# Masked cross attention: the key stack as two 64-row halves, three stacks in rotation, unrolled rounds

## The chip, the cores and the metric

The kernel runs on one NeuronCore of a Trainium2 chip, as one program in one launch. The metric is the device time of one execution in microseconds. TensorE (PE, with its weight loads as PEld) multiplies into PSUM; VectorE (DVE), ScalarE (ACT) and GpSimd (POOL) read PSUM and SBUF; SyncE (SP) only issues DMA transfers, all of them in one queue. Each engine works through its own instructions in order and waits on semaphores.

## The reference, cut to what matters

The program is a two-layer perceiver block over 16 batches of 64 tokens with 128 channels. The change touches one stage, the masked cross attention of layer 1 (`L1_xattn`), and the buffers around it:

```python
q = split_heads(x @ cq_w + cq_b)            # x: 16 x 64 x 128, 16 heads of 8
k = split_heads(ctx @ ck_w + ck_b)          # ctx: 16 x 1601 x 128
v = split_heads(ctx @ cv_w + cv_b)
scores = einsum('bqhd,bkhd->bhqk', q, k) / sqrt(8) + mask      # mask: 16 x 1 x 1 x 1601
probs = softmax(scores, axis=-1)
out = einsum('bhqk,bkhd->bqhd', probs, v)
```

The other stages (cross attention and self attention of layer 0, expert networks, self attention, quantised attention) are left as they are.

## The kernel before, in words

Everything of the stage is done per batch. The keys of a batch (128 channels x 1601) are projected in four chunks (512, 512, 512, 65 columns) and split into a rounded part `kh` (ACT) and a rest `kl` (DVE), so that fast fp32r multiplications keep fp32 accuracy. A stack `KS` (128 partitions x 4 groups x 1602) then holds, for each group g of four heads, `kh`, `kh` and `kl` of the group's 32 channels in partitions 0 to 95, and above them rows for the maximum and the mask. The queries are stacked in the same way (`QS`) and spread over heads by POOL (`QB`). One multiplication of a stack with `QB` gives scores that include mask and minus the maximum.

For each batch two passes over the scores are made. The first gives maxima: 8 head pairs x 4 key chunks = 32 matmuls in the layout queries x keys, each into PSUM bank 0 or 1 in turn, each reduced by one DVE instruction (line 1516). The maxima of a batch are then combined, transposed on PE (`nm`, line 1264), split into `nmh` and `nml` and sent by two small DMAs (line 897) into two rows of `QB`. The second pass gives scores in the layout keys x queries, 13 tiles of keys (steps k = 0 to 12): four matmuls into a pair of banks (2-3 or 4-5 in turn), one exponential on ACT into `PT` (line 1112), and eight column-tiled matmuls with the values (`values`).

The stage runs in slots n = -2 to 16, each of 13 steps. In slot n, PE does step k of batch n, and beside it the maxima of batch n+1 (0, 0, 3, 4, 4, 4, 4, 4, 4, 5, 0, 0, 0 of them in steps 0 to 12), and one side task per step through bank 7: `sum` of batch n-1 in step 1 (DVE takes its reciprocal, line 1499), the value projections `v0` to `v3` of batch n+1 in steps 2 to 5, the key projections `k0` to `k3` of batch n+2 in steps 6 to 9, and `nm` in step 10. A side task waits until bank 7 has been read by the one before it.

There are two stacks, `KS0` and `KS1`. The stack of batch n+1 is filled in slot n by SP (`sync_slot`): when the last scores of batch n-1 are done, one mask transfer and twelve transfers of 32 partitions x 1601 elements, in the order of the groups (`kh`, `kh`, `kl` for g = 0, then for g = 1, and so on); PE waits for a group before that group's first maximum. Behind them in SP's queue stand the load of the next context into `ctxT` and then the two small maxima transfers. Slots 2 to 11 are a loop of five rounds (`Fori`) with register arithmetic for semaphore values and addresses; the others are written out.

Of the kernel before, what the change touches and what calls it, by code (L numbers as in the profile page):

```python
# [16 lines left out]
HEADS, HD = 16, 8  # L17
# [36 lines left out]
def build(nc, A, out, mask_parts):  # L54
    ctx = ExitStack()
    with ctx:
# [25 lines left out]
        W["L1_xattn_fi_w"] = sb("w_fi", [128, FF])  # L82
        W["L1_xattn_fo_w"] = sb("w_fo", [128, FC, 128])
# [11 lines left out]
        for name in ("L0_xattn_bv", "L1_xattn_sv_b", "L1_xattn_co_b", "L1_xattn_co_g", "L1_xattn_co_be",  # L95
# [11 lines left out]
        qT = sb("qT", [128, 128])  # L107
# [16 lines left out]
        WqT = sb("WqT", [128, 128])  # L124
        WvT = sb("WvT", [128, 128])
# [3 lines left out]
        pc_sb = sb("pc_sb", [128, 128])  # L129
        pcT = sb("pcT", [128, 128])  # L130
# [33 lines left out]
        onT = expert_area[:, 0:2 * TOKENS].rearrange("p (r t) -> p r t", r=2)  # L164
# [6 lines left out]
        split_x = [q[:, :] for q in QB]  # L171
# [23 lines left out]
        LANE[0].update(q=qT[:, :], smax=smax[:, :], ssum=ssum[:, :])  # L195
        LANE[1].update(q=o_sb[:, :], smax=sb("smax1", [128, HEADS])[:, :], ssum=sb("ssum1", [128, HEADS])[:, :])
# [530 lines left out]
        MAXIMA = [(p, c) for p in range(8) for c in CS]  # L727
# [6 lines left out]
        progress("max_p", [f"m{p}{c}" for p, c in MAXIMA] + ["nm"])  # L734
        progress("max_v", [f"m{p}{c}" for p, c in MAXIMA] + ["nm", "nmh", "nml"])
# [15 lines left out]
        mask_stacked = sem("mask_stacked")  # L751
        ctxT_loaded = [sem(f"ctxT_loaded{q}") for q in range(2)]
        qs_stacked = sem("qs_stacked")
        ks_stacked = [sem(f"ks_stacked{g}") for g in range(4)]
        nm_stacked = sem("nm_stacked")
        mask_split = sem("mask_split")
# [27 lines left out]
        for name, t in W.items():  # L784
            src = A[name]
            if name == "L1_xattn_fo_w":
                src = src.rearrange("(c p) n -> p c n", p=128)
            elif name == "L1_attn_in_w":
                src = src.rearrange("(c p) n -> p c n", p=128)
            WLOADS.append((t, src))  # L790
# [11 lines left out]
        def slots(eng, slot):  # L802


            for n in (-2, -1, 0, 1):
                slot(n, n % 2)
            with eng.Fori(0, 5) as i:
                slot(2 * i + 2, 0)
                slot(2 * i + 3, 1)
            for n in (12, 13, 14, 15, 16):  # L810
                slot(n, n % 2)

        BESIDE = {k: ([], None) for k in range(KT)}
        for k, side, count in SCHEDULE:
            first = sum(len(b[0]) for b in BESIDE.values())
            maxima = ["m%d%d" % MAXIMA[m] for m in range(first, first + count)]
            BESIDE[k] = (maxima, side)
        IN_BANK7 = ["sum", "v0", "v1", "v2", "v3", "k0", "k1", "k2", "k3", "nm"]  # L820

        def present(item, n):
            c = isinstance(n, int)
            if item == "sum":
                return not (c and n < 1)
            if item[0] == "k":
                return not (c and n > 13)
            return not (c and (n < -1 or n > 14))

        def maxima(n, k, part=None):  # L830

            m = [item for item in BESIDE[k][0] if present(item, n)]
            return m if part is None else (m[:2], m[2:])[part]

        def side(n, k):

            item = BESIDE[k][1]
            return [item] if item and present(item, n) else []

        def bank7_free(item, n):  # L840

            before = [b for b in IN_BANK7[:IN_BANK7.index(item)] if present(b, n)]
            if before:
                last, m = before[-1], n
            elif isinstance(n, int) and n == 16:
                last, m = "sum", 15
            elif isinstance(n, int) and n == -1:
                last, m = "k3", -2
            elif isinstance(n, int) and n < -1:
                return  # L850
            else:
                last, m = "nm", n - 1
            if last == "sum":
                at(nc.tensor, "sum_v", "sum", m - 1)
            elif last[0] == "v":
                at(nc.tensor, "vals_a", last, m + 1)
            elif last[0] == "k":
                at(nc.tensor, "keys_v", "kl" + last[1], m + 2)
            else:
                at(nc.tensor, "max_v", "nml", m + 1)  # L860
# [13 lines left out]

        def sync_slot(n, q):

            c = isinstance(n, int)
            if not (c and n > 14):
                stack = KS[1 - q]
                if c and n <= 0:  # L880
# [798 lines left out]
```

## Time and profile before

| what | value |
|---|---|
| median of 3 runs | 1426.14 us (1424.24 to 1427.14) |
| the profiled execution | 1429.34 us, its span 1427.6 us |
| PE busy | 1091.4 us (76%) |
| DVE busy | 759.6 us (53%) |
| ACT busy | 482.5 us (34%) |
| POOL busy | 227.4 us (16%) |
| hardware DMA queue | 96.48 MB, 25.2% of 16 engines' span |
| chain of waits | PE 49%, issue 18%, DVE 14%, SP's queue 6%, DMA 5%, POOL 5%, ACT 2% |

The stage of the change reaches from about 412 us (the last expert result of layer 0) to about 1027 us of the span. The table is an average over all stages; within the slots PE is busy about nine tenths of the time at full clock, and the DMA engines are busy in the first 13 us of a slot's 34 and nearly idle in the rest. A busy PE row counts matmuls from issue to modelled end, so it is not PE at its peak.

### The profile page before, as it was taken

The page shows a single profiled execution, that of the slowest core. Times are in us where ns is not written, and L with a number is a line of the kernel's source. Part 1 is how long each engine was busy: PE and PEld are TensorE (multiplying, and loading weights), DVE is VectorE, ACT ScalarE, POOL GpSimd, SP SyncE. Part 2 cuts the span into 40 slices and gives each one's busy share as a digit, 9 for nine tenths or more (in the row PEclk, how much of TensorE's full clock was granted, in tenths as well). Part 3 has the DMA queues.
Part 4 walks back from the last instruction along what each step waited for, and adds up shares of the span by engine and source line. Part 5 has one row for each costly group of instructions (what it writes and reads, how often), then busy time and mean ns, then how long its engine had stood idle before and what let it go on. Part 6 is the DMA issues. An engine that isn't in the chain of part 4 may idle for free.

```text
span 1427.6 us, 24169 instructions
## 1 busy us (share of the span) xinstructions
PE 1091.4 (76%) x9246; PEld 795.1 (56%) x9246; DVE 759.6 (53%) x1498; ACT 482.5 (34%) x632; POOL 227.4 (16%) x232
## 2 busy tenths in 40 slices
PE   3677774899862798988898888988758625838987
PEld 1445463777741466666666666666536413536776
DVE  3224766343342566666666666666176377955112
ACT  0225221232220245455445455554414101402333
POOL 2000412121221011111111111111133003301110
PEclk9889876999985799999999999999879766857999
DMA  8581010101104344443444343433000000010111
GB/s 270 209 326 52 1 44 1 45 22 44 68 0 105 90 103 99 97 95 94 98 111 94 94 94 94 94 72 72 2 0 1 1 0 1 0 30 16 30 30 29
DMA packets 43611, 97.30 MB, mean 68 GB/s; under 512 B 12392, under 2 KB 27376, under 8 KB 43552
## 3 DMA queue, kind: packets, MB, share of 16 engines
q1 hardware_dynamic: 43552, 96.48, 25.2%
q8 instruction: 42, 0.69, 0.2%
q14 instruction: 17, 0.14, 0.0%
HBM read 54.67 MB, written 0.73 MB: 39 GB/s over the span
## 4 chain that ended last, share of the span: by engine, by line
PE 49%; issue 18%; DVE 14%; SPq 6%; DMA 5%; POOL 5%; ACT 2%; DVEq 0%; POOLq 0%; ACTq 0%
PE PS L262 47%; DVE mx L1516 3%; DMA KS<-kl 3%; DVE kl L1505 2%; SPq L913 2%; POOL work_area L390 2%; DVE u_all L275 1%; SPq L897 1%; DMA ctxT<-in_ctx_T 1%; POOL PT L390 1%; SPq L889 1%; DVE x L675 1%; DMA QB<-nml 1%; POOL blank_g L257 1%; POOL rstd_all L281 1%
## 5 line engine op out<-in xcount | busy, mean ns | idle before, releaser
L1516 DVE TENSOR_REDUCE mx<-PS 128x1 f32<-128x512 f32 (+1 forms) x512 | 278.5, 571 | 100.5 <-PE PS L262 93.0
L1112 ACT ACTIVATE PT<-PS 128x1024 f32<-128x1024 f32 (+1 forms) x208 | 212.4, 1022 | 64.6 <-PE PS L262 64.6
L262 PE MATMUL PS<-KS,QB 128*128 128x512 f32 (+1 forms) x512 | 178.8, 419 | 41.0 <-DVE mx L1516 22.0
L262 PE MATMUL PS<-QB,KS 128*128 128x256 f32 (+1 forms) x832 | 166.7, 323 | 18.1 <-DMA QB<-nml 18.1
L262 PE MATMUL PS<-QB,QS 128*128 128x512 f32 x576 | 157.5, 421 | 23.9 <-DVE wcol L663 21.7
L262 PEld LDWEIGHTS PS<-QB,KS 128*128 128x128 f32 (+1 forms) x832 | 116.8, 189 | 51.9 <-issue 28.1
L262 PEld LDWEIGHTS PS<-QB,QS 128*128 128x128 f32 x576 | 108.5, 199 | 60.6 <-issue 26.9
L262 PEld LDWEIGHTS PS<-KS,QB 128*128 128x128 f32 x512 | 90.2, 191 | 93.0 <-issue 46.5
L675 DVE SCALAR_TENSOR_TENSOR x<-PS,wcol,x 128x128 f32<-128x128 f32 x128 | 44.9, 351 | 136.8 <-PE PS L262 133.4
L292 PE MATMUL PS<-consts,u_all 128*128 128x128 f32 x64 | 15.7, 427 | 97.6 <-DVE u_all L275 77.0
L1098 ACT ACTIVATE kh<-PS,c_L_xattn_ck_b 128x512 fp32r<-128x512 f32 x64 | 38.1, 595 | 147.4 <-PE PS L262 123.5
L1499 DVE RECIPROCAL prT<-PS 128x256 f32<-128x256 f32 x16 | 28.1, 1758 | 109.1 <-PE PS L262 109.1
L262 PE MATMUL PS<-expert_area,work_area 128*128 128x128 f32 (+2 forms) x720 | 72.8, 276 | 11.3 <-DVE work_area L670 5.9
L654 ACT ACTIVATE work_area<-PS 128x512 f32<-128x512 f32 x64 | 38.3, 598 | 126.5 <-PE PS L262 126.5
L262 PEld LDWEIGHTS PS<-expert_area,work_area 128*128 128x128 f32 (+2 forms) x720 | 70.4, 176 | 16.0 <-DVE work_area L670 7.6
L262 PE MATMUL PS<-ctxT,w_L_xattn_ck_w 128*128 128x512 f32 (+1 forms) x128 | 61.2, 560 | 23.3 <-DVE kl L1505 23.3
L257 POOL TENSOR_TENSOR blank_g<-consts 128x1 f32<-128x1 f32 x54 | 20.7, 384 | 344.3 <-PE PS L262 244.5
L262 PE MATMUL PS<-PT,work_area 128*32 128x128 f32 (+1 forms) x1664 | 68.3, 283 | 2.4 <-ACT prT L1118 2.1
L262 PE MATMUL PS<-PT,early 128*32 128x128 f32 (+1 forms) x1664 | 67.3, 280 | 2.4 <-ACT prT L1118 1.9
L292 PEld LDWEIGHTS PS<-consts,u_all 128*128 128x128 f32 x64 | 12.6, 224 | 99.4 <-DVE u_all L275 52.3
L262 PEld LDWEIGHTS PS<-expert_area,PT 128*128 128x128 f32 x512 | 59.5, 192 | 1.4
L262 PE MATMUL PS<-expert_area,PT 128*128 128x128 f32 x512 | 59.8, 275 | 0.0
(240 smaller groups left out, 1578.7 us busy)
## 6 DMA issues: line engine op xcount, KB each, us to landing
KS<-kh SPq DMA_DIRECT2D x128, 200.1 KB, 4.1
ctxT<-in_ctx_T SPq DMA_DIRECT2D x24, 800.5 KB, 4.7
KS<-kl SPq DMA_DIRECT2D x64, 200.1 KB, 4.0
early<-in_ctx_tiles SPq DMA_DIRECT2D x8, 832.0 KB, 8.0
expert_area<-in_ctx_tiles SPq DMA_DIRECT2D x8, 832.0 KB, 6.3
work_area<-in_ctx_T SPq DMA_DIRECT2D x8, 800.5 KB, 10.5
expert_area<-in_L_ffn_experts_w SPq DMA_DIRECT2D x24, 256.0 KB, 3.2
expert_area<-in_L_ffn_W SPq DMA_DIRECT2D x16, 256.0 KB, 3.0
```

The lines of the kernel that those rows point to most:

```text
L257: nc.gpsimd.tensor_tensor(blank_g[:, k:k + 1], consts[:, 0:1], consts[:, 0:1], ALU.mult)
L262: return T.matmul(o, l, r, start=start, stop=stop, **k)
L292: last = T.transpose(PS[:, 512 * (6 + h) + 128 * t:512 * (6 + h) + 128 * t + 128], src[:, 4 * h + t, :], ident)
L390: return eng.tensor_tensor(dst[:, 1024 * g:1024 * g + 1024].rearrange("p (h k) -> p h k", h=HEADS), src, hm, ALU.mult)
L654: ins = S.activation(g_act[:, c % 2, :], bank(2 * (c % 2)), ACT.Silu)
L675: last = V.scalar_tensor_tensor(x[:, 4 * t + q, :], PS[:, 512 * (4 + t) + q * 128:512 * (4 + t) + (q + 1) * 128], wcol[:, j, 4 * t + q:4 * ...
L913: sp.dma_start(dst, src).then_inc(loads, 16)
L1098: P["keys_a"].done(S.activation(kh[:, c0:c0 + cw], bank(7, cw), ACT.Identity, bias=COLS["L1_xattn_ck_b"][:, 0:1]), f"kh{c}")
L1112: P["exp_a"].done(S.activation(PT[0:rows, par, :], PS[0:rows, 1024 + 1024 * par:2048 + 1024 * par], ACT.Exp), f"e{k}")
L1499: P["sum_v"].done(V.reciprocal(rsum, bank(7, 256)), "sum")
L1505: P["keys_v"].done(V.scalar_tensor_tensor(kl[:, c0:c0 + cw], bank(7, cw), COLS["L1_xattn_ck_b"][:, 0:1], kh[:, c0:c0 + cw], ALU.add, ALU.s ...
L1516: P["max_v"].done(V.reduce_max(mx[:, p, c:c + 1], bank((4 * p + c) % 2, CHUNKS[c][1]), AX), item)
```

## The change

The stack is laid out in two halves of 64 rows. Half a holds head pair a of each of the four groups: 16 rows `kh`, 16 rows `kh`, 16 rows `kl`, and the maximum and mask rows at 48 to 51 (the maximum only in half 0). The weights and biases of the query and key projections are permuted beforehand so that channels come in this order. A maxima step j now issues two matmuls, one on rows 0 to 63 and one on rows 64 to 127, into two different banks (0-1 or 4-5 in turn), and one DVE reduction reads both (128 x 2 x 512). Twelve such steps and a thirteenth for the four short chunks (8 matmuls of 66 columns, one reduction) replace 32 matmuls and 32 reductions. The scores keep all 128 rows in one matmul, but have a single pair of banks (2-3): the scores of a step wait for the exponential of the step before.

There are three stacks and three `QB`. The third stack lies in the area of the layer-0 context tiles and experts, the second value buffer moves, `onT` is split in two, and the two feed-forward weights of layer 1 are loaded at the end of the stage, since `QB2` lies in their place. The stack of batch n+2 is filled in slot n: two mask transfers, then, once `kh3` is there, four `kh` transfers of 16 x 4 x 1601 elements (64 source partitions each), and once `kl3` is there, two for `kl`. Keys are projected in steps 1 to 4, `sum` is in step 5, values in steps 6 to 9, `nm` in step 10; the first two maxima steps of batch n+2 stand in steps 11 and 12 of slot n, and the first of them waits for the whole stack. All slots are written out.

```diff
-SCHEDULE = ((1, "sum", 0), (2, "v0", 3), (3, "v1", 4), (4, "v2", 4), (5, "v3", 4), (6, "k0", 4),
-            (7, "k1", 4), (8, "k2", 4), (9, "k3", 5), (10, "nm", 0))
+MAX_STEPS = ([2], [3], [4], [5], [6], [7, 8], [9], [10, 11], [12], [], [], [0], [1])
+SIDES = (None, "k0", "k1", "k2", "k3", "sum", "v0", "v1", "v2", "v3", "nm", None, None)
...
+        def maxima_banks(b, j):
+            o = 2048 * ((N_MAX * b + j) % 2)
+            return PS[:, o:o + 1024].rearrange("p (a k) -> p a k", a=2)
+
+        def stacked(eng, b):
+            eng.wait_ge(ks_stacked[b % 3], 128 * (b // 3 + 1))
...
-                stack = KS[1 - q]
-                if c and n <= 0:
-                    at(nc.sync, "keys_v", "kl3", n + 1)
-                else:
-                    at(nc.sync, "exp_p", f"s{KT - 1}", n - 1)
-                nc.sync.dma_start(stack[98:100, :, :].bitcast(F32),
-                                  mask_parts[:, bass.ds(n + 1, 1), :].broadcast_to([2, 4, KPAD])).then_inc(mask_stacked, 16)
-                for g in range(4):
-                    for k, src in enumerate((kh, kh, kl)):
-                        nc.sync.dma_start(stack[32 * k:32 * k + 32, g, 0:KEYS].bitcast(F32),
-                                          src[32 * g:32 * g + 32, 0:KEYS].bitcast(F32)).then_inc(ks_stacked[g], 16)
+            b = n + 2
+            if b < BATCH:
+                stack = KS[b % 3]
+                if b >= 3:
+                    at(nc.sync, "exp_p", f"s{KT - 1}", b - 3)
+                for a in range(2):
+                    nc.sync.dma_start(stack[64 * a + 50:64 * a + 52, :, :].bitcast(F32),
+                                      mask_parts[:, b:b + 1, :].broadcast_to([2, 4, KPAD])).then_inc(ks_stacked[b % 3], 16)
+                for k, src in enumerate((kh, kh, kl)):
+                    if k == 0:
+                        at(nc.sync, "keys_a", "kh3", b)
+                    if k == 2:
+                        at(nc.sync, "keys_v", "kl3", b)
+                    for a in range(2):
+                        nc.sync.dma_start(stack[64 * a + 16 * k:64 * a + 16 * k + 16, :, 0:KEYS].bitcast(F32),
+                                          src[64 * a:64 * a + 64, 0:KEYS].bitcast(F32)).then_inc(ks_stacked[b % 3], 16)
...
-            for g in range(4):
-                for k, src in enumerate((qh, ql, qh)):
-                    sp.dma_start(QS[32 * k:32 * k + 32, g, :].bitcast(F32), src[32 * g:32 * g + 32, :].bitcast(F32)
-                                 ).then_inc(qs_stacked, 16)
+            for k, src in enumerate((qh, ql, qh)):
+                for a in range(2):
+                    sp.dma_start(QS[64 * a + 16 * k:64 * a + 16 * k + 16, :, :].bitcast(F32),
+                                 src[64 * a:64 * a + 64, :].bitcast(F32)).then_inc(qs_stacked, 16)
...
+            def maximum(b, j):
+                if j == 0:
+                    at(T, "qb_g", "qb", b)
+                    stacked(pe, b)
+                if N_MAX * b + j >= 2:
+                    free = N_MAX * b + j - 2
+                    at(T, "max_v", f"m{free % N_MAX}", free // N_MAX)
+                out = maxima_banks(b, j)
+                for g in ([j // 3] if j < 12 else range(4)):
+                    for a in range(2):
+                        rows, p = slice(64 * a, 64 * a + 64), 2 * g + a
+                        c0, cw = CHUNKS[j % 3 if j < 12 else 3]
+                        o = cw * g if j == 12 else 0
+                        last = mm(out[:, a, o:o + cw], QB[b % 3][rows, 128 * p:128 * p + 128], KS[b % 3][rows, g, c0:c0 + cw])
+                P["max_p"].done(last, f"m{j}")
...
-                        if k >= 2:
-                            at(T, "exp_a", f"e{k - 2}", n)
-                        elif not (c and n < 1):
-                            at(T, "exp_a", f"e{k + KT - 2}", n - 1)
+                        if k >= 1:
+                            at(T, "exp_a", f"e{k - 1}", n)
+                        elif n >= 1:
+                            at(T, "exp_a", f"e{KT - 1}", n - 1)
                         for g in range(4):
-                            o = 1024 + 1024 * par + 256 * g
-                            last = mm(PS[0:rows, o:o + 256], KS[q][:, g, 128 * k:128 * k + rows], QB[q][:, 256 * g:256 * g + 256])
+                            o = 1024 + 256 * g
+                            last = mm(PS[0:rows, o:o + 256], KS[n % 3][:, g, 128 * k:128 * k + rows], QB[n % 3][:, 256 * g:256 * g + 256])
...
+            sp.dma_start(fi_w, A["L1_xattn_fi_w"]).then_inc(ffn_loaded, 16)
+            sp.dma_start(fo_w, A["L1_xattn_fo_w"].rearrange("(c p) n -> p c n", p=128)).then_inc(ffn_loaded, 16)
```

SP's queue in one slot of the loop before. `KS1` is the stack of the next batch, `QB1` its queries; the two pieces of a row are the transfer and its size.

```order
L885 ISA [waits exp_p]
L885 DMA KS1<-mask_parts 2x4x1602
L889 DMA KS1<-kh 32x1601 x2
L889 DMA KS1<-kl 32x1601
L889 DMA KS1<-kh 32x1601 x2
L889 DMA KS1<-kl 32x1601
L889 DMA KS1<-kh 32x1601 x2
L889 DMA KS1<-kl 32x1601
L889 DMA KS1<-kh 32x1601 x2
L889 DMA KS1<-kl 32x1601
```

The same queue in one slot now. `KS2_49` is the third stack, filled for the batch after the next; `QB1` belongs to the next batch.

```order
L862 DMA KS2_49<-mask_parts 2x4x1602 [waits exp_p]
L862 DMA KS2_49<-mask_parts 2x4x1602
L870 DMA KS2_49<-kh 16x4x1601 [waits keys_a]
L870 DMA KS2_49<-kh 16x4x1601 x3
L870 DMA KS2_49<-kl 16x4x1601 [waits keys_v]
L870 DMA KS2_49<-kl 16x4x1601
L852 DMA ctxT<-in_ctx_T 128x1601 [waits vals_p]
L878 DMA QB1<-nmh 1x8x128 [waits max_v]
L878 DMA QB1<-nml 1x8x128 [waits max_v]
```

Twelve transfers into 32 partitions that started with the slot have become six into 16 partitions that start when the slot's key projections are done. The context load and the two maxima transfers still stand behind them.

PE's instructions around the end of a slot before (`KS0`, `QB0` are of the batch whose steps 11 and 12 these are; `nm_stacked` is the arrival of the maxima of the next batch).

```order
L262 MATMUL PS<-QB0,KS0 128x256 x3
L221 REGISTER_ALU
L262 MATMUL PS<-PT,work_area 32x128 [waits exp_a]
L262 MATMUL PS<-PT,work_area 32x128 x7
L262 MATMUL PS<-QB0,KS0 65x256 [waits exp_a]
L262 MATMUL PS<-QB0,KS0 65x256 x3
L221 REGISTER_ALU
L262 MATMUL PS<-PT,work_area 32x128 [waits exp_a]
L262 MATMUL PS<-PT,work_area 32x128 x7
L1304 REGISTER_ALU
L262 MATMUL PS<-QB1,KS1 128x256 [waits exp_a,nm_stacked]
```

The same place now: steps 11 and 12 of the batch in `KS1`, with the first two maxima steps of the batch in `KS0` (two batches on from the one before it in the rotation), then step 0 of the batch in `KS2_49`.

```order
L262 MATMUL PS<-QB1,KS1 128x256 x3
L262 MATMUL PS<-KS0,QB0 128x512 [waits max_v,ks_stacked0,qb_g]
L262 MATMUL PS<-KS0,QB0 128x512
L262 MATMUL PS<-PT,work_area 32x128 [waits exp_a]
L262 MATMUL PS<-PT,work_area 32x128 x7
L262 MATMUL PS<-QB1,KS1 65x256 [waits exp_a]
L262 MATMUL PS<-QB1,KS1 65x256 x3
L262 MATMUL PS<-KS0,QB0 128x512 [waits max_v]
L262 MATMUL PS<-KS0,QB0 128x512
L262 MATMUL PS<-PT,work_area 32x128 [waits exp_a]
L262 MATMUL PS<-PT,work_area 32x128 x7
L262 MATMUL PS<-QB2_50,KS2_49 128x256 [waits exp_a,nm_stacked]
```

A wait for a whole stack (`ks_stacked0`) now stands in PE's order in step 11, ahead of the values of step 10 and of everything of step 12. Before, the waits for the stack's groups stood in steps 2 and later of the next slot.

## Rows read from the trace of the kernel before

**Rows 1.** Groups by shape, 693 to 967 us (eight slots); columns as on the page

```profile
L1516 DVE TENSOR_REDUCE mx<-PS 128x1 f32<-128x512 f32 x192 | 126.5, 687 | 18.8 <-PE PS L262 14.7
L1112 ACT ACTIVATE PT<-PS 128x1024 f32<-128x1024 f32 x97 | 99.1, 1022 | 23.8 <-PE PS L262 23.8
L262 PE MATMUL PS<-KS,QB 128*128 128x512 f32 x192 | 80.0, 471 | 10.9 <-DMA KS<-kl 8.3 <-DVE mx L1516 2.6
L262 PE MATMUL PS<-QB,KS 128*128 128x256 f32 x384 | 77.7, 324 | 8.1 <-DMA QB<-nml 8.1
...
L1516 DVE TENSOR_REDUCE mx<-PS 128x1 f32<-128x66 f32 x64 | 14.3, 224 | 23.2 <-PE PS L262 23.2
L1499 DVE RECIPROCAL prT<-PS 128x256 f32<-128x256 f32 x8 | 14.1, 1758 | 50.3 <-PE PS L262 50.3
```

**Rows 2.** Timeline of DVE: combined maxima in slots 0 and 13

```profile
520.12 0.18 DVE L1509 TENSOR_REDUCE nm<-mx 128x8 f32<-128x32 f32 x1
...
965.42 0.18 DVE L1509 TENSOR_REDUCE nm<-mx 128x8 f32<-128x32 f32 x1
```

**Rows 3.** Timeline: one key chunk, from its matmul to the next one's

```profile
645.61 1.02 PE L262 MATMUL PS<-ctxT,w_L_xattn_ck_w 128*128 128x512 f32 x2
...
646.88 0.69 ACT L1098 ACTIVATE kh<-PS,c_L_xattn_ck_b 128x512 fp32r<-128x512 f32 x1 [2.24 <-PE PS L262]
...
648.09 0.74 DVE L1505 SCALAR_TENSOR_TENSOR kl<-PS,c_L_xattn_ck_b,kh 128x512 fp32r<-128x512 f32 x1
...
648.89 1.13 PE L262 MATMUL PS<-ctxT,w_L_xattn_ck_w 128*128 128x512 f32 x2 [0.16 <-DVE kl L1505]
```

**Rows 4.** Timeline: step 11 of a slot, scores, exponential, values, next scores

```profile
657.83 0.54 PEld L262 LDWEIGHTS PS<-QB,KS 128*128 128x128 f32 x4
...
658.61 1.03 ACT L1112 ACTIVATE PT<-PS 128x1024 f32<-128x1024 f32 x1 [0.23 <-PE PS L262]
...
659.08 0.42 PEld L262 LDWEIGHTS PS<-QB,KS 128*65 128x65 f32 x4 [0.20 <-issue]
...
659.69 0.38 PEld L262 LDWEIGHTS PS<-PT,work_area 128*32 128x32 f32 x16 [0.19 <-ACT PT L1112]
```

**Rows 5.** Timeline of SP: the stack's last transfer in a slot

```profile
670.23 1.02 SPq L889 DMA_DIRECT2D KS<-kl  x1
```

**Rows 6.** Windows: PE, PEld, DVE, ACT, POOL busy; granted clock; DMA share; GB/s

```profile
46.00:48.00 2.00, 0.00 (x0) 0.00 (x0) 0.00 (x0) 0.00 (x0) 0.00 (x0) 1.00 0.89 103
51.00:53.00 2.00, 0.00 (x0) 0.00 (x0) 0.00 (x0) 0.00 (x0) 0.00 (x0) 0.50 1.01 419
454.00:458.00 4.00, 0.00 (x0) 0.00 (x0) 0.00 (x0) 0.00 (x0) 0.00 (x0) 0.50 1.01 213
666.00:673.00 7.00, 6.79 (x81) 5.17 (x81) 5.42 (x10) 3.05 (x5) 2.50 (x6) 1.00 1.02 220
```

**Rows 7.** Timeline: the stage's start, from the query stack to slot 0's scores

```profile
430.66 0.63 SPq L942 DMA_DIRECT2D QS<-kh  x1
...
440.09 0.69 ACT L1098 ACTIVATE kh<-PS,c_L_xattn_ck_b 128x512 fp32r<-128x512 f32 x1 [23.91 <-DMA QS<-kh]
...
451.95 0.32 ACT L1098 ACTIVATE kh<-PS,c_L_xattn_ck_b 128x65 fp32r<-128x65 f32 x1 [1.57 <-PE PS L262]
...
452.94 1.15 SPq L889 DMA_DIRECT2D KS<-kh  x2
...
458.49 0.50 PEld L262 LDWEIGHTS PS<-KS,QB 128*128 128x128 f32 x2 [6.76 <-issue]
...
489.75 1.78 PEld L262 LDWEIGHTS PS<-QB,KS 128*128 128x128 f32 x8 [3.60 <-DMA QB<-nml]
```

**Rows 8.** Window: the clock 12 us after PE took up dense work

```profile
470.00:472.00 2.00, 1.74 (x6) 0.99 (x6) 1.12 (x3) 0.60 (x1) 0.00 (x0) 0.53 0.00 0
```

**Rows 9.** Timeline: first and last scores of slot 15

```profile
1002.97 0.53 PEld L262 LDWEIGHTS PS<-QB,KS 128*128 128x128 f32 x4 [0.74 <-DMA QB<-nml]
...
1018.61 0.43 PEld L262 LDWEIGHTS PS<-QB,KS 128*65 128x65 f32 x4 [0.20 <-issue]
```

More of the change, by code:

```diff
@@ L800, in build @@
         N_W = len(WLOADS) + 16
[L802 to L833, printed above, removed]
+        def slots(slot):
+            for n in range(-2, BATCH + 1):
+                slot(n)
@@ L835, in side, with maxima @@
+        def maxima(n, k):
+            b = n + 1 if k < 11 else n + 2
+            return [(b, j) for j in MAX_STEPS[k]] if 0 <= b < BATCH else []
+        SIDE_OF = {"k": 2, "v": 1, "n": 1, "s": -1}
         def side(n, k):
[L837 to L842, printed above, removed]
+            item = SIDES[k]
+            return item if item and 0 <= n + SIDE_OF[item[0]] < BATCH else None
@@ L843, in bank7_free @@
+        def bank7_free(k, n):
+            before = [(m, i) for m in range(-2, n + 1) for i in range(KT) if side(m, i) and (m, i) < (n, k)]
             if before:
[L844 to L850, printed above, removed]
-            else:
-                last, m = "nm", n - 1
@@ L853, in bank7_free @@
[L853 to L860, printed above, removed]
+                m, i = before[-1]
+                item = SIDES[i]
+                b = m + SIDE_OF[item[0]]
+                if item == "sum":
+                    at(nc.tensor, "sum_v", "sum", b)
+                elif item[0] == "v":
+                    at(nc.tensor, "vals_a", item, b)
+                elif item[0] == "k":
+                    at(nc.tensor, "keys_v", "kl" + item[1], b)
+                else:
+                    at(nc.tensor, "max_v", "nml", b)
@@ L1315, in slot @@
-                    if k and not (c and (n < 0 or n > 15)):
-                        values(n, k - 1, q)
-                    if k == 0 and not (c and n < 1):
-                        values(n - 1, KT - 1, 1 - q)
-                    for item in maxima(n, k, 1) + side(n, k):
-                        beside(item, n, q)
-            slots(pe, slot)
+                    for b, j in maxima(n, k)[:1]:
+                        maximum(b, j)
+                    if k and 0 <= n < BATCH:
+                        values(n, k - 1)
@@ L1324, in _ @@
+                    if k == 0 and n >= 1:
+                        values(n - 1, KT - 1)
+                    for b, j in maxima(n, k)[1:]:
+                        maximum(b, j)
+                    if side(n, k):
+                        beside(k, n)
+            slots(slot)
             at(T, "fin_g", "on", BATCH - 1)
```

271 lines of the change are left out of this document (126 added, 145 removed).

## The prediction

> **What bounds the kernel now.** I read the groups by shape of eight slots first, then one slot's timeline, then the DMA windows. PE is never long without work, but waits in three places: for DVE's reductions, for the last key transfer (8.3 us in eight slots) and for the maxima transfer (8.1) [rows 1]. DVE spends 126.5 + 14.3 us on maxima and ACT 99 us on exponentials in these 274 us, so neither is full. A slot lasts (965.42 - 520.12) / 13 = 34.25 us [rows 2]. Its long steps are those of the key projections: from one chunk's matmul to the next's 3.28 us, namely 1.27 to `kh`, 0.69 `kh`, a wait until DVE is free of two reductions, 0.74 `kl` [rows 3]. A step with nothing beside it takes 659.08 - 657.83 = 1.25 us [rows 4]. The stack's last transfer of a slot is issued by 671.25 [rows 5], 10 us into the slot, and the DMA engines are full until then (share 1.02, 220 GB/s) [rows 6]; PE stalls little on them, since the groups come in the order of their use.
>
> **Part by part.** Times below are from one execution, 1429.34 us with a span of 1427.6; the median is 3.2 us lower.
>
> *Maxima on DVE.* A reduction takes 687 ns for 512 columns and 224 for 66 [rows 1], 1.04 ns per column and a fixed 0.16 us; 1024 columns then take 1.22 us. Per slot 24 x 0.687 + 8 x 0.224 = 18.3 us become 12 x 1.22 + 0.7 = 15.3. DVE is not the bound, so this counts only where it shortens the key chain: one reduction, done before `kh` is, leaves 1.27 + 0.69 + 0.05 + 0.74 + 0.06 = 2.8 us per chunk for 3.28.
>
> *Maxima on PE.* 24 x 512 columns at 2.4 GHz are 5.1 us of streaming in a slot, 41 of the 80.0 us that rows 1 show for eight slots. If two row halves run together, half of it goes, 2.6 us; if not, nothing. Almost all of it lies in steps that end on something else, so I take 0 to 1.
>
> *One pair of banks for the scores.* From the start of scores to the exponential 0.78 us, the exponential 1.03, release 0.05 [rows 4]: a step is now at least 1.86 us. This replaces 1.25 in steps 0, 9, 11, 12 and about that in 10: some +3 us, against which the wait for `nml` (1.0 us a slot) goes, since steps 10 to 12 now cover its 3.5 us.
>
> *The slot if no transfer were late.* Time 0 is the matmul of `k0`, 1.5 us into step 1. `k3` comes at 3 x 2.8 = 8.4; step 5 starts at 8.8, holds two maxima steps, and `sum`; its reciprocal (1.76 us) stands behind reductions and ends near 14.4, which holds `v0` in step 6; steps 7, 8, 9 start at 15.5, 18.2, 21.1, and at 1.86 each step 10 at 23.1, 11 at 24.9, 12 at 26.8, 0 at 28.6, 1 at 30.5, next `k0` at 32.0. That would be 2.3 us less than now.
>
> *The stack's transfers.* This decides. `kh3` is ready at 8.4 + 0.8 = 9.2. The first bytes move 1.1 us after the issue (issue at 452.94 [rows 7], full rate from 454.0 [rows 6]) and the last are seen about 1.7 us after they moved (600 KB at 213 GB/s from 454.0 end at 456.8; PE goes at 458.49). The first maxima step wants the stack at 24.9 + 0.5 = 25.4. So 6 x 64 x 6404 bytes = 2.46 MB have 25.4 - 1.7 - 10.3 = 13.4 us, and need 184 GB/s. Transfers into 32 partitions run at 213 to 220 GB/s with the engines full; context loads into 128 partitions at 419 with the engines just as full; and the two saves of the mask, out of 16 partitions, 200 KB, ran at 103 GB/s with a share of 0.89 [rows 6]. The rate goes with the number of partitions touched, two to one in the first pair and again in the second, and every transfer of the new stack writes 16. Bounds: 213 GB/s (11.5 us; its source has 64 partitions now) and 100 GB/s (24.6 us). I take 107, near the row with 16 partitions: 23.0 us.
>
> The Trainium skill says this outright ("SBUF — State Buffer", on the DMA port swizzle): partitions 0 to 15 reach 4 of 16 ports and it measured 104 GB/s, 0 to 31 reach 8 with 189, all 128 reach 16 with 328. The trace agrees in its ratios, with 103, 213 and 419. By the page's 104 the stack would take 23.6 us in place of my 23.0, 9 us more over the kernel.
>
> *The slot with it.* The last byte is there at 10.3 + 23.0 = 33.3, seen at 35.0. PE has stood since 25.4 with the values of step 10, scores of step 12 and all later work queued behind. Then one maxima step and values, 1.1, to step 12; 1.86 to step 0; 1.86 to step 1; 1.5 to `k0`: 41.3. The context load (0.8 MB, 2.0 us at 419 GB/s) and the two maxima transfers stand behind the stack and land 3.9 us after its last byte, just as step 0 wants them (4.6). PE's idle stretch of nearly 10 us lets the granted clock fall: after the 6.8 us wait at 458.49 it was still 0.53 at 470 to 472, with PE 87% busy [rows 8], so steps 12, 0 and part of the keys run at 1.2 GHz. I add 1.5 (0 to 3). Period 42.8, that is +8.55 us in each of the 14 slots 0 to 13 that fill a stack: +119.7.
>
> *Start.* The query stack (1.57 MB, also into 16 partitions now) takes 14.7 for 7.4 us: +7.4 on the 440.09 of rows 7. `kh3` of batch 0 is then ready at 459.7, the whole stack at 459.7 + 1.1 + 23.0 + 1.7 = 485.5, where PE now starts at 458.49 with a quarter of it. Four maxima steps 3.6, the cold key chain 12.2 (440.09 to 452.27), then 1.1 + 23.0 for batch 1: 525.4, and slot 0's scores wait for the maxima behind it, 529.3 in place of 489.75 [rows 7]: +39.6. Counting the period from the stack's last byte adds 0.7. The fill of the third stack on ACT (6408 columns, some 5.7 us) runs before 430 beside the normalisation and costs 0, or 6 if that cover fails.
>
> *End.* Slot 14 projects no keys and waits for no stack: about 28.7 for 34.1 us, -5.4. Slot 15 has nothing beside its scores: 15.64 us from first to last [rows 9] become 12 x 1.86 = 22.3, +6.7. The unrolled code takes away some register rows; slots in the loop and outside it differ by 0.3 us at most, so 0 to -2. Late feed-forward weights are covered by self attention, 0.
>
> Sum: 119.7 + 39.6 + 0.7 - 5.4 + 6.7 = +161. 1429.3 + 161 = 1590.6, as a median 1587 us.
>
> **Rivals.**
>
> *The transfers keep today's rate.* Then no stall; slots of 32.0: -2.3 x 14 = -32; the start costs +9.5 (whole stack instead of a quarter), the end +1.3: 1405. For it: the source is 64 partitions, the halves alternate between transfers, and before there is no transfer into 16 partitions in the stage. Against it: the 103 GB/s. This is the side of faster; it decides from 184 GB/s up.
>
> *The engines spread over several transfers.* Within a transfer 16 engines crowd on few partitions; if some run ahead into the next, which lies in the other half, both are served at once. With 18 us for the stack, 5 us less in 16 stacks and 3 in the query stack: 1504. For it: the 103 GB/s window has a share of 0.89 only, so that its engines were not all held up at once. Against it: before, `kh` and `kl` also alternate halves and the rate stays at 213 to 220. The Trainium skill ("SBUF — State Buffer", on issuing two DMAs for both halves) gives only 6% for two such transfers at once; by that the stack would take 21.7 us.
>
> *Fast transfers, but the row halves gain nothing and cost switches of the array's shape.* PE would pay 12 x 0.21 us for pairs that run one after the other and, at some 0.2 us (the issue gaps of rows 4), about 13 more gaps in a slot, half of both hidden: slots of 34.6 and with start and end about 1442. The Trainium skill ("TensorEngine Tiling (Array Packing)", key properties) says a change of tiling mode drains TensorE; the values are column-tiled already, so most steps switch today, and the gap of 0.20 behind them is all the trace shows.
>
> **How the numbers follow.** Forecast 0.66, today's rate 0.15, spread engines 0.13, switches 0.06. The forecast's own range is 1540 to 1640: 100 GB/s and 3 us of cold clock add 3.1 us in 16 slots, a slightly faster 115 GB/s and no clock loss take as much. Down to 1450 it takes in the spread engines and part of the rest: 1450 to 1640. A measurement tells 0.2%, 3 us, from no change; today's rate is the only case clearly faster, so faster 0.16, same 0.02, slower 0.82.
>
> **What would show it.** Right: PE's largest wait is for `KS<-kl`, some 8 to 10 us in each slot at step 11; DMA windows in slots at full share with 100 to 115 GB/s; a period of `nm` near 43; granted clock below 1 after each wait; the new reduction at 1.22 us. Wrong: a rate of 180 GB/s or more, no wait at step 11, a period near 32; or a period near 35 with PE's gaps grown. Also wrong, by the small terms, if scores follow each other in slot 15 at other than 1.86 us.

## The result and the profile after

The changed kernel takes 1593.46 us (median of 4 runs, 1576.77 to 1595.84), the kernel before 1426.64 (median of 4 runs): a ratio of 1.113, with a 95% interval of 1.107 to 1.119. The profiled execution took 1595.84 us, with a span of 1594.1, 166.5 more than before.

The groups by line of the changed kernel, from its page (busy and mean ns, then the idle time ahead of them):

```profile
L1495 DVE TENSOR_REDUCE mx<-PS 128x2 f32<-128x1024 f32 x192 | 230.6, 1218 | 263.6 <-PE PS L262 263.5
L1087 ACT ACTIVATE PT<-PS 128x1024 f32<-128x1024 f32 (+1 forms) x208 | 212.3, 1020 | 263.4 <-PE PS L262 263.4
L262 PE MATMUL PS<-KS,QB 64*128 64x512 f32 (+1 forms) x512 | 122.9, 510 | 166.4 <-issue 139.9
L262 PE MATMUL PS<-QB,KS 128*128 128x256 f32 (+1 forms) x832 | 184.3, 348 | 17.3 <-ACT PT L1087 15.3
```

DVE and ACT both stood 263 us, and for PE. PE's own idle time lies ahead of the maxima, 166 us. These rows put most of it down to "issue", that is to nothing the profile shows. Of the waits for a stack the view of waits names only that of the second batch (total, times, longest):

```profile
PE PS L262 <- issue: 143.4, 22, 13.4
PE PS L262 <- DMA KS<-kl: 24.5, 1, 24.5
```

So the others have to be found in one slot. Its timeline (start, duration, engine and operation, idle time before it in brackets), first as above [rows 3], then around step 11:

```profile
834.35 1.13 PE L262 MATMUL PS<-ctxT,w_L_xattn_ck_w 128*128 128x512 f32 x2
...
837.04 1.13 PE L262 MATMUL PS<-ctxT,w_L_xattn_ck_w 128*128 128x512 f32 x2
...
843.23 4.42 SPq L870 DMA_DIRECT2D KS<-kh  x4
...
847.69 1.98 SPq L870 DMA_DIRECT2D KS<-kl  x2
...
847.92 1.16 PE L262 MATMUL PS<-w_L_xattn_cv_w,ctxT 128*128 128x128 f32 x8 [1.02 <-DVE prT L1484]
...
856.21 0.37 SPq L852 DMA_DIRECT2D ctxT<-in_ctx_T  x1
...
867.33 0.79 PE L262 MATMUL PS<-KS,QB 64*128 64x512 f32 x2 [8.37 <-issue]
...
877.61 1.81 PE L262 MATMUL PS<-ctxT,w_L_xattn_ck_w 128*128 128x512 f32 x2
```

Keys follow each other at 2.69 us; the stack's transfers are all issued by 849.67; and from 858.96 PE stands 8.37 us and restarts with the first maxima step of the next stack. The windows of the same slot and of the start (columns as in [rows 6]) show what it waits for:

```profile
846.00:862.00 16.00, 11.42 (x141) 8.41 (x141) 6.76 (x9) 7.72 (x10) 2.19 (x4) 1.00 1.00 112
862.00:866.00 4.00, 0.00 (x0) 0.00 (x0) 0.00 (x0) 0.00 (x0) 0.00 (x0) 0.50 1.07 121
866.00:868.00 2.00, 0.67 (x2) 0.32 (x2) 0.00 (x0) 0.00 (x0) 0.00 (x0) 0.50 0.79 272
430.00:441.00 11.00, 0.00 (x0) 0.00 (x0) 0.00 (x0) 0.00 (x0) 0.00 (x0) 0.50 0.91 101
464.00:476.00 12.00, 0.00 (x0) 0.00 (x0) 0.00 (x0) 0.00 (x0) 0.00 (x0) 0.50 0.98 108
```

The DMA engines are full, with 112 GB/s where the same share gave 220 before. At about 866, when 2.46 MB at 112 GB/s from 844.3 are through, the rate jumps (the context load stands behind the stack), and PE goes on. The period, from slots 0 and 13 as in [rows 2], is (1111.70 - 544.40) / 13 = 43.64 us, for 34.25:

```profile
544.40 0.19 DVE L1501 TENSOR_REDUCE nm<-mx 128x8 f32<-128x32 f32 x1
...
1111.70 0.18 DVE L1501 TENSOR_REDUCE nm<-mx 128x8 f32<-128x32 f32 x1
```

The 166.5 us by these stamps: the stage's start up to slot 0's `nm` +24.3, thirteen periods +122.0, from slot 13's `nm` to the last scores of slot 15 +16.2 (53.19 became 1181.11 - 1111.70), behind that +4.0.

### The profile page after: what moved, and what is told of

Same layout as the page of the kernel before. It is cut to its first block, busy times and chain, and to the rows that moved or that the text cites. A ratio compares the mean times of both kernels' runs of the same rounds, so it can differ in the third digit from the quotient of the medians.

```text
span 1594.1 us, 22366 instructions
## 1 busy us (share of the span) xinstructions
PE 1120.3 (70%) x9246; PEld 789.6 (50%) x9246; DVE 724.3 (45%) x1194; ACT 489.1 (31%) x633; POOL 222.9 (14%) x202
## 4 chain that ended last, share of the span: by engine, by line
PE 46%; issue 22%; DVE 12%; ACT 7%; POOL 4%; DMA 4%; SPq 3%; POOLq 0%; DVEq 0%
PE PS L262 45%; ACT PT L1087 3%; DVE mx L1495 2%; DVE kl L1478 2%; ACT kh L1074 2%; DVE prT L1484 2%; POOL work_area L390 2%; SPq L894 2%; DVE u_all L275 1%; DMA KS<-kl 1%; DMA ctxT<-in_ctx_T 1%; DMA QB<-nml 1%; POOL PT L390 1%; DMA QS<-kh 1%; DVE x L675 1%
## 5 line engine op out<-in xcount | busy, mean ns | idle before, releaser
L1495 DVE TENSOR_REDUCE mx<-PS 128x2 f32<-128x1024 f32 x192 | 230.6, 1218 | 263.6 <-PE PS L262 263.5
L262 PE MATMUL PS<-KS,QB 64*128 64x512 f32 (+1 forms) x512 | 122.9, 510 | 166.4 <-issue 139.9
L262 PE MATMUL PS<-PT,work_area 128*32 128x128 f32 (+1 forms) x3328 | 152.9, 308 | 0.5 <-ACT PT L1087 0.5
L262 PEld LDWEIGHTS PS<-KS,QB 64*128 64x128 f32 x512 | 50.7, 209 | 206.8 <-issue 182.1
L262 PEld LDWEIGHTS PS<-QB,QS 128*128 128x128 f32 x576 | 110.6, 203 | 61.8 <-issue 27.6
L262 PEld LDWEIGHTS PS<-PT,work_area 128*32 128x32 f32 (+1 forms) x3328 | 87.8, 119 | 53.8 <-issue 45.1
L262 PE MATMUL PS<-nat_area,work_area 128*128 128x128 f32 (+2 forms) x928 | 85.0, 275 | 13.6 <-DVE work_area L670 5.9
L262 PEld LDWEIGHTS PS<-nat_area,work_area 128*128 128x128 f32 (+2 forms) x928 | 81.8, 167 | 19.0 <-DVE work_area L670 7.6
L262 PE MATMUL PS<-w_L_xattn_cv_w,ctxT 128*128 128x128 f32 (+1 forms) x416 | 63.8, 293 | 14.9 <-DVE prT L1484 14.1
L1478 DVE SCALAR_TENSOR_TENSOR kl<-PS,c_L_xattn_ck_b,kh 128x512 fp32r<-128x512 f32 x64 | 40.5, 633 | 61.8 <-ACT kh L1074 61.7
L262 PEld LDWEIGHTS PS<-w_L_xattn_cv_w,ctxT 128*128 128x128 f32 (+1 forms) x416 | 50.7, 190 | 29.9 <-DVE prT L1484 17.8
```

The lines of the kernel that those rows point to most:

```text
L262: return T.matmul(o, l, r, start=start, stop=stop, **k)
L1478: P["keys_v"].done(V.scalar_tensor_tensor(kl[:, c0:c0 + cw], bank(7, cw), COLS["L1_xattn_ck_b"][:, 0:1], kh[:, c0:c0 + cw], ALU.add, ALU.s ...
L1495: ins = V.reduce_max(by_pair[:, :, j // 3, j % 3:j % 3 + 1], src, AX)
```

## The experiments

The first question was what makes the stack's transfers slow. The number alone, 112 GB/s for a forecast 107, did not show that its reason was right.

**Control without mask rows, and 32 destination partitions.** In both the two mask transfers are left out; the second also writes each 64-partition source into 32 partitions of two groups instead of 16 of four. The stacks of the second, and of the two further kernels without mask rows that place rows elsewhere, don't hold what the queries ask for; only their times are read. Long arguments are shortened in the code from here on.

```diff
-  nc.sync.dma_start(stack[64 * a + 16 * k:64 * a + 16 * k + 16, :, 0:KEYS].bitcast(F32),
+  r0, g0 = 64 * a + (32 if k == 2 else 0), 2 * (k % 2)
+  nc.sync.dma_start(stack[r0:r0 + 32, g0:g0 + 2, 0:KEYS].bitcast(F32),
                     src[64 * a:64 * a + 64, 0:KEYS].bitcast(F32))
```

> The changed kernel without the two mask transfers of each stack (the mask rows are left out of the scores), everything else as it is: six transfers of 16 partitions x 4 groups. This is the control for the next kernel. Theory (the stack's transfers are slow because each writes only 16 partitions): the masks go out at the start of a slot, when the engines are idle, so nothing changes: 1585 to 1600 us, windows in the transfers at about 112 GB/s, a wait of 9 us at step 11. Rival (the doubled mask transfers, which move little through two partitions, hold the queue up): 20 us or more faster.

> As the control, but each of the six transfers writes 32 partitions x 2 groups instead of 16 x 4: the same sources, the same 64 rows of 6404 bytes, the same number of transfers and the same place in the queue; the stack's contents are then not those of the reference. Theory (number of partitions written decides): rate 213 to 220 GB/s, the stack takes 11.5 us instead of 22, the wait at step 11 is gone, the period of a slot is near 32 and the time 1405 to 1425 us, the query stack still being slow (+7). Rival A (the 64 source partitions, or transfers of 400 KB, are slow): rate and time as in the control, 1590. Rival B (engines spread over transfers of both halves, some gain only): 150 GB/s, 1480 to 1510.

The control took 1583.32 us (ratio 1.110, 1.104 to 1.117), a little below the range expected and not separated from the changed kernel's 1.113, with 110 GB/s in the window 846 to 850. With 32 destination partitions it was 1557.78 (1.092, 1.087 to 1.098). The window of the latter:

```profile
788.00:800.00 12.00, 8.57 (x111) 6.42 (x109) 3.81 (x6) 5.99 (x8) 0.41 (x2) 1.00 1.03 120
```

Twice the destination partitions gave 120 GB/s, not 213. The number of partitions written, the reason in my prediction, doesn't decide. What is left is the source of 64 partitions, or that a transfer folds several source partitions into one.

**64 into 64, 16 into 16, and 32 folded into 16.** One edit each: the control with all 64 partitions of a half written to the same 64 of one group; the kernel before with each 32-partition transfer split in two of 16; the control with twelve transfers from 32 partitions into 16 of two groups.

```diff
+  nc.sync.dma_start(stack[64 * a:64 * a + 64, k, 0:KEYS].bitcast(F32), src[64 * a:64 * a + 64, 0:KEYS])
...
+  nc.sync.dma_start(stack[32 * k + 16 * s:32 * k + 16 * s + 16, g, 0:KEYS].bitcast(F32),
+                    src[32 * g + 16 * s:32 * g + 16 * s + 16, 0:KEYS].bitcast(F32))
...
+  nc.sync.dma_start(stack[64 * a + 16 * k:64 * a + 16 * k + 16, g:g + 2, 0:KEYS].bitcast(F32),
+                    src[64 * a + 16 * g:64 * a + 16 * g + 32, 0:KEYS].bitcast(F32))
```

> The changed kernel without the mask rows (its control without them took 1583 us), in which each of the six transfers of a stack copies 64 partitions into the same 64 partitions of one group, not into 16 partitions of four groups; the stack's contents are then wrong, its bytes and row lengths (6404 bytes) are the same. Theory A (folding 64 source rows into fewer partitions is what slows them, as 64 into 32 ran at about 120 GB/s): 200 GB/s or more and 1395 to 1425 us. Rival B (a 64-row source is slow, with four neighbouring rows for each of the 16 engines): 110 to 125 GB/s and 1550 to 1590 us.

> The kernel before, complete, with each of the twelve 32-partition transfers of a stack split into two of 16 rows into 16 partitions, unfolded: 24 transfers of 102 KB, so 6 us more of SP's issuing (12 more of 0.49 us). Theory A (16 destination partitions are slow by themselves): about 107 GB/s, 23 us per stack, PE waits for it, 1490 to 1515 us. Rival B (only folding is slow): rate near the 213 GB/s of before, 1426 to 1440 us.

> The changed kernel without the mask rows (control 1583 us), in which twelve transfers each copy 32 source partitions into 16 partitions of two groups (two rows of 6404 bytes to a partition) instead of six of 64 into 16 of four. Theory A (a transfer that folds several source partitions into one partition is slow; 64 into 32 ran at 120 GB/s, 64 into 64 and 32 into 32 above 200): 110 to 130 GB/s and 1540 to 1590 us. Rival B (only a 64-partition source together with a narrower destination is slow): 160 GB/s or more and 1400 to 1450 us.

They took 1402.34 us (ratio 0.981, 0.977 to 0.985), 1457.98 (1.019, 1.016 to 1.023) and 1565.53 (1.095, 1.089 to 1.101). One window of each, in this order, inside the stack's transfers:

```profile
734.00:740.00 6.00, 4.99 (x58) 3.61 (x56) 4.92 (x5) 2.54 (x3) 2.20 (x4) 1.00 0.99 225
```

```profile
741.00:755.00 14.00, 11.89 (x119) 9.19 (x112) 7.11 (x11) 6.10 (x8) 2.49 (x6) 0.88 0.88 162
```

```profile
704.00:720.00 16.00, 10.14 (x122) 7.64 (x121) 4.45 (x7) 6.76 (x9) 1.85 (x4) 0.90 1.03 124
```

Every unfolded transfer is fast: 225 GB/s from 64 partitions. Sixteen into sixteen reach 162, at a share of 0.88: SP takes 2.46 us to issue four of them,

```profile
739.34 2.46 SPq L890 DMA_DIRECT2D KS<-kh  x4
```

which is 102 KB per 0.61 us, 167 GB/s, so issuing holds them back. That is not all of it: with full engines 162 / 0.88 gives 184 GB/s, an estimate, still below the 213 to 220 of 32 into 32. Every folded transfer is slow, 112, 120 and 124 GB/s, whether two or four rows go to a partition and whether 32 or 64 are read. So the folding costs the factor of two. One thing goes with it in all three: a folded row also changes its place within a block of 32 partitions, while the unfolded rows here keep theirs. The stepped transfers below move rows without folding and stay fast, but they spread over all 128 partitions; rows reordered within 32 partitions, unfolded, weren't tried. For the 16 into 16, at 1457.98 us, both stated theories missed (1490 to 1515 and 1426 to 1440): 16 partitions were not slow at 107, and were not free either.

**The whole new schedule on the stacks of before.** Three stacks, paired reductions, one pair of score banks and written-out slots are kept; maxima run on 128 rows, and the twelve transfers of 32 into 32 partitions are back.

```diff
-  rows, p = slice(64 * a, 64 * a + 64), 2 * g + a
+  rows, p = slice(0, 128), 2 * g + a
...
+  for g in range(4):
+      nc.sync.dma_start(stack[32 * k:32 * k + 32, g, 0:KEYS].bitcast(F32), src[32 * g:32 * g + 32, 0:KEYS])
```

> The changed kernel with the stacks of the kernel before: 128-row maxima matmuls (no row halves), 32-partition transfers, twelve to a stack, one mask transfer, no permuted weights; paired reductions, single score banks, three stacks, the order of steps and the unrolling stay. Theory: the transfers run at 213 to 220 GB/s and are there before step 11; the period is 32.0 plus at most 2.6 for maxima matmuls that stream twice as long, mostly hidden; start +9, end +1: 1395 to 1425 us, so the row halves are what costs 170 us and all the rest together gains 0 to 30. Rival (the schedule with early maxima and single score banks is itself slow): 1440 us or more.

1404.24 us (0.984, 0.980 to 0.988), with 218 GB/s and a period of 31.6:

```profile
762.00:770.00 8.00, 6.97 (x74) 5.66 (x72) 6.40 (x5) 3.35 (x5) 2.20 (x4) 1.00 1.01 218
```

PE's waits for "issue" are down to 8.7 us in all, from 143.4. That is the case that the prediction held as its first rival, 1405 with slots of 32.0. Everything in the change but the stack's layout makes the kernel 22 us faster; the layout gives back 189.

**Unrolling alone,** on the kernel before.

> The kernel before with the slot loop written out, nothing else changed. Theory: the loop's jumps lie in waits; 0 to 3 us less (ratio 0.998 to 1.0). Rival: the 22 us that the kernel with full rows gains come largely from unrolling, ratio 0.985 to 0.992.

1429.97 us, ratio 0.9995 (0.997 to 1.002): no change, as expected.

**Hiding the slow transfers: maxima later, and the maxima's transfer on another queue.** The first stack-dependent maxima step moves from step 11 to step 2 of the next slot; the second kernel also has POOL issue `nmh` and `nml` on its own queue.

```diff
-MAX_STEPS = ([2], [3], [4], [5], [6], [7, 8], [9], [10, 11], [12], [], [], [0], [1])
+MAX_STEPS = ([], [], [0], [1], [2, 3], [4, 5], [6, 7], [8, 9], [10, 11], [12], [], [], [])
...
-  nc.sync.dma_start(QB[(n + 1) % 3][48 + k:49 + k, :], src[:, :])
+  nc.gpsimd.dma_start(QB[(n + 1) % 3][48 + k:49 + k, :], src[:, :])
```

> The changed kernel with all thirteen maxima steps of a batch in steps 2 to 9 of the slot before its own, none in steps 11 and 12 of the slot before that; transfers untouched. Theory (the cost lies in where the wait stands, not only in the rate): PE asks for the stack 9 us later, keys of the next batch are no longer queued behind the wait, and the period is that of the buffer kh, which ACT may not overwrite before the stack has been copied: 1.1 + 22 + 1.7 us of transfer and 7.9 from the first to the last key chunk, 33 to 34 us. With the slow start kept (+36 us) about 1450 us, between 1435 and 1475. Rival (the rate alone decides and the wait only moves): above 1560 us.

> The changed kernel, complete, with its slow folded transfers and with the maxima of the next batch from step 2 on (1563 us), and with the two transfers of the negated maxima issued by POOL on its own queue instead of SP's behind the stack and the context. Theory: there only the order within SP's queue delays them; beside it they take their share of the 16 engines and land before the next slot, the wait of 7.6 us goes, period 33 to 36 and 1425 to 1480 us. Rival: the engines are full with the stack's rows whatever queue asks, the two small transfers land no earlier, 1550 us or more.

They took 1563.28 us (1.097, 1.092 to 1.101) and 1566.89 (1.096, 1.090 to 1.102): the rival was right both times. The timelines around the next slot's first scores, of the one and of the other:

```profile
713.24 0.69 SPq L878 DMA_DIRECT2D QB<-nmh  x1
...
713.98 0.69 SPq L878 DMA_DIRECT2D QB<-nml  x1
...
723.87 1.22 PE L262 MATMUL PS<-QB,KS 128*128 128x256 f32 x4 [7.59 <-DMA QB<-nml]
```

```profile
758.25 0.56 POOL L880 DMA_DIRECT2D QB<-nmh  x1 [8.60 <-DVE nmh L1493]
758.81 0.52 POOL L880 DMA_DIRECT2D QB<-nml  x1
...
768.14 1.22 PE L262 MATMUL PS<-QB,KS 128*128 128x256 f32 x4 [4.01 <-DMA QB<-nml]
```

The 4 KB of `nml` need 9 to 10 us from issue to use in either queue, as long as the 16 engines are still at the stack's rows and the context behind them. The wait moved; it didn't shrink below what the transfers take: PE's waits for `nml` add up to 110.6 us in the one and 112.7 in the other, with periods of 41.6 us in both. With no stack in transit the same POOL transfer is quick, so it isn't slow by its queue. The first line is of slot 14, which fills no stack (window 1120 to 1132, the last figure is the time from issue to landing); the second is over all 32 of the run:

```profile
QB<-nml POOLq DMA_DIRECT2D x1, 4.0 KB, 1.6
```

```profile
DMA to landing us min/median/max: 1.6/9.6/11.6
```

My expectation for the first had left out that all later small transfers share those engines.

**Row halves without folding.** Copy k of channel i of a group goes to partition 4i + k. Channels 0 to 15 of each group are then in the lower half and 16 to 31 in the upper, and each transfer is 32 into 32 partitions, four apart. The maximum and mask rows move to partitions 3, 7, 11 and 15; the weights aren't permuted. The second kernel also swaps one reduction from step 5 to step 6, and a third does that to the kernel with full rows.

```diff
+  for g in range(4):
+      nc.sync.dma_start(stack[k:128:4, g, 0:KEYS].bitcast(F32), src[32 * g:32 * g + 32, 0:KEYS].bitcast(F32))
...
-  c[:, C_QM:C_QM + 4] = (half == j // 2) & ((row >= 48) | ((row % 16) // HD == j % 2))
+  c[:, C_QM:C_QM + 4] = (half == j // 2) & ((row % 4 == 3) | ((row // 4) // HD == j % 2))
...
-MAX_STEPS = ([2], [3], [4], [5], [6], [7, 8], [9], [10, 11], [12], [], [], [0], [1])
+MAX_STEPS = ([2], [3], [4], [5], [6], [7], [8, 9], [10, 11], [12], [], [], [0], [1])
```

> The changed kernel, complete, with its row halves kept, but the twelve key and query transfers of a stack as wide as before: 32 source rows into 32 partitions, one each. For that the rows of the stack are interleaved: copy k of channel i of a group lies in partition 4i+k, so that channels 0 to 15 of a group fall in the lower half and 16 to 31 in the upper half by themselves, the maximum and the mask lie in partitions 3, 7, 11, 15 (and 67 to 79), and the projections need no permutation. Theory A (the narrow or folded transfers alone cost the time): stack at 200 to 220 GB/s, no wait for it in step 11, period 31 to 32, whole kernel 1385 to 1410 us, and at or a little below the 1404 us of the kernel with full rows, since a pair of 64-row maxima takes 0.5 us of PE instead of 0.8 twice. Rival B (any two-half layout makes the transfers slow, since their partitions lie far apart): 110 to 130 GB/s and 1550 us or more. Rival C (pairs of 64-row matmuls drain PE between tilings): transfers fast, but a period of 33 to 34 and 1425 to 1445 us.

> The kernel with interleaved rows (1398.5 us, period 31.0), with one maxima step in step 5 and two in step 6, instead of two in step 5 and one in step 6. In its trace the reciprocal of the sums starts at 731.49, behind two reductions, though the sum's matmuls start at 730.10; v0 waits 1.02 us for it. Theory: with one reduction ahead the reciprocal starts near 730.8, v0 0.6 to 0.7 us earlier, and 15 slots give 9 to 10 us: 1386 to 1392 us. Rival: the second reduction of step 6 now lies behind the reciprocal, and the matmuls of steps 6 and 7 that want its banks wait as long: 1396 to 1401 us.

> The kernel with full rows (128-row maxima, stack and transfers as before, three stacks, paired reductions; 1404.2 us, period 31.6), complete, with one maxima step in step 5 and two in step 6. With interleaved row halves the same edit gave 1384.1 us. Theory: the halves are worth what the two periods before the edit show, 31.64 - 31.02 = 0.6 us a slot, 9 us in all: 1389 to 1395 us. Rival: with the reciprocal out of the way PE's time alone sets the period, and the halves, which take about 0.3 us from each of 13 maxima steps, are worth 2 us or more a slot: 1405 us or more. Second rival: they are worth nothing, 1382 to 1387 us.

1398.53 us (0.979, 0.976 to 0.981), 1384.12 (0.968, 0.965 to 0.971) and 1388.43 (0.971, 0.969 to 0.973). The second, complete, is faster than both kernels compared here. The window of the first, then the reciprocal and `v0` in the second:

```profile
730.00:740.00 10.00, 8.98 (x103) 7.00 (x102) 7.57 (x8) 4.05 (x5) 2.19 (x4) 1.00 0.94 224
```

```profile
724.93 1.23 DVE L1495 TENSOR_REDUCE mx<-PS 128x2 f32<-128x1024 f32 x1 [0.16 <-PE PS L262]
...
726.13 1.76 DVE L1484 RECIPROCAL prT<-PS 128x256 f32<-128x256 f32 x1
...
727.95 1.16 PE L262 MATMUL PS<-w_L_xattn_cv_w,ctxT 128*128 128x128 f32 x8
```

Spread over 128 partitions, 32-partition transfers run at 224 GB/s. In the second, `v0` no longer waits for the reciprocal (1.02 us before), and the period (mean of the 15 from slot -1 to 14) falls from 31.02 to 30.22 us, 12 us in all; 14.4 were timed and 9 to 10 expected. The third lies just under its range, at 1388.43 for 1389 to 1395. The two pairs with halves and with full rows differ by 5.7 and 4.3 us, with intervals that overlap in both, so the halves' own worth is a few microseconds and not separated from none. The traces, one of each, agree with a few: over the same 15 periods 31.57 us with full rows and 31.02 with halves, then 30.51 and 30.22. Groups by shape from 620 to 868 us, with halves and with full rows, show what PE gains:

```profile
L262 PE MATMUL PS<-KS,QB 64*128 64x512 f32 x192 | 48.0, 496 | 0.0
```

```profile
L262 PE MATMUL PS<-KS,QB 128*128 128x512 f32 x190 | 61.2, 403 | 0.0
```

The halves take 13 us less of PE in eight slots, 1.7 in a slot (the two rows hold nearly the same count), but the period fell by 0.5. The rest must lie in steps that end on something else, the score banks, the key chain or DVE; which of them takes how much I haven't worked out.

## Why the prediction came out right, point by point

**What decides.** Forecast: the stack is late for step 11, PE stands there and the granted clock falls. So it is in every slot that fills a stack, and 1587 us against 1593.46. One sign that I named doesn't show as I wrote it: the largest wait is not labelled `KS<-kl` but "issue", though it stands in step 11, at 8.4 to 10.6 us in slots 0 to 13.

**The step that was right in number and wrong in its reason** is "The rate goes with the number of partitions touched". That its number came out is luck. The 16 destination partitions were not what halved the rate: unfolded transfers into 16 ran at 162 GB/s, folded ones into 32 at 120. I had taken 107 from a window of a save from SBUF to HBM [rows 6], another kind of transfer, and three rows that lay on one line made it look like a law. The 103 GB/s was not a steady rate either, but the 205 KB of both saves over the 2 us that I had cut around them; 1.5 us hold nearly the same bytes:

```profile
46.25:47.75 1.50, 0.00 (x0) 0.00 (x0) 0.00 (x0) 0.00 (x0) 0.00 (x0) 1.00 1.15 132
```

The cause is the fold, as far as the runs separate it. By my reason, 32 destination partitions would have mended the kernel; they gave 26 us of some 180. The Trainium skill's rule on the port swizzle ("SBUF — State Buffer") states 104 GB/s for 16 partitions; the 162 here is against it for a stream of SBUF-to-SBUF transfers that write different sets of 16 in turn (as those of the changed kernel do, at 112), and the measurement decides. Nor do the ratios agree as I wrote: 103, 213 and 419 double with the page's counts of ports, 4, 8 and 16, but the page's measured 104, 189 and 328 do not. Why folding costs so much no run here shows; that a transfer folded on both its sides would be slow too wasn't tried.

**The stall.** From `k0` to PE's restart at step 11 I had 35.0 us; 834.35 to 867.33 is 33.0, the shortest; all fourteen slots 0 to 13 lie between 33.0 and 34.9, with a mean of 34.1: 112 GB/s for 107.

**The cold clock** was the mis-sized term of the period. From the restart to the next `k0` I had 6.3 and 1.5 for the clock. In 8 of 13 slots it took 10.3 (867.33 to 877.61), in 5 between 7.6 and 8.4. The windows behind one such restart:

```profile
870.00:874.00 4.00, 4.00 (x33) 2.36 (x36) 1.40 (x2) 1.92 (x2) 1.89 (x1) 0.50 0.10 24
874.00:878.00 4.00, 4.00 (x39) 2.52 (x32) 2.28 (x2) 1.53 (x3) 0.00 (x0) 0.50 0.01 2
878.00:882.00 4.00, 3.90 (x27) 1.97 (x27) 1.82 (x2) 1.60 (x2) 0.00 (x0) 0.87 0.00 0
```

PE is busy without a gap from 870 to 878, at 1.2 GHz. Where the way to `k0` was short the clock was back sooner, as after the restart at 997.91:

```profile
1000.00:1002.00 2.00, 2.00 (x22) 1.20 (x20) 0.51 (x2) 1.02 (x1) 1.16 (x1) 0.52 0.04 6
1002.00:1004.00 2.00, 1.95 (x34) 1.09 (x22) 1.34 (x2) 1.02 (x1) 0.73 (x1) 1.00 0.12 35
```

The mean of the thirteen is 9.4 us, so the term is 3.1 instead of 1.5, and with the restart 0.9 us earlier the period came to 43.64 for 42.8, +11 us over thirteen.

**The start** was 9 us too dear: slot 0's scores came at 520.17, not 529.3. The stage itself began 4.9 us earlier (query stack issued at 425.74, [rows 7] 430.66), which I didn't foresee and haven't followed up; the query stack took 6.4 us more for 7.4, the two stacks some 3 less between them. **The end** held: +16.2 us from slot 13's `nm` to the last scores, where the forecast's terms leave 16.7 (the fourteenth period 8.6, the end 1.3, the 0.7, and 6.1 because `nm` now comes 24.23 and not 30.37 us after a slot's first scores). The 4 us behind the stage I had at 0. The misses -9, +11 and +4 partly cancel, which is luck too.

**The slot without a stall.** 32.0 was predicted, 31.6 is the period with full rows. The row halves' gain on PE, which I had at 0 to 1 us a slot, is 0.5 and 0.3 in the two pairs of traces. Reductions of 1.22 us and key chunks at 2.69 for 2.8 are as worked out, and so is the pace of bare scores, in slot 15:

```profile
1177.40 0.74 PE L262 MATMUL PS<-QB,KS 128*128 128x256 f32 x4 [0.54 <-ACT PT L1087]
...
1179.26 0.74 PE L262 MATMUL PS<-QB,KS 128*128 128x256 f32 x4 [0.54 <-ACT PT L1087]
```

1.86 us, to the digit. No gap of a changed tiling shows in PE's rows: the pairs of 64 rows have 0.0 us of idle time ahead of them in the groups above.

**The rivals.** Today's rate (0.15) is what the unfolded kernels do. Spread engines (0.13) and costly switches (0.06) were not met.

## What to carry to other kernels

Lay out an SBUF-to-SBUF copy so that each source partition lands in a partition of its own; interleave rows with a step rather than pack several into one partition. A rate read from one kind of transfer doesn't price another: when three rows lie on a line, ask which other property they share. And before moving a consumer away from a late transfer, list the small transfers that share its engines, since they will be late next.

## What the hardware showed unexpectedly

- Folding 64 into 16, 64 into 32 and 32 into 16 partitions ran at 112, 120 and 124 GB/s with the engines full; 64 into 64, 32 into 32 and 32 into every fourth partition at 225, 218 and 224, with the same 6404-byte rows. 16 into 16 reached 162 at a share of 0.88.
- A 4 KB transfer on POOL's queue took as long to land as one on SP's behind full engines (9.3 us from 758.81 to its use at 768.14), where the same transfer took 1.6 in the slot without a stack to fill.
- After a wait of 8.4 us PE ran at half clock to 878, 11 us on, although it was busy throughout; after another of 8.7 us the granted clock was back at 1.00 some 4 us on (997.91 to 1002). After five of the thirteen waits PE took some 2 us less than after the others to reach the next `k0`.
